# Attention edges: a drain between two chained sums in place of a semaphore's update and wait

## The chip, the cores and the metric

The kernel runs on one core of a Trainium2 chip. The metric is the device time of one execution in microseconds (us). The kernel before was run three times; the median is 8269.03 us.

## What is computed

A graph of 12500 nodes and 200000 edges, sorted by their target node, passes through an equivariant message layer and then through two graph attention layers. The change lies in the edge loop of the attention layers, which runs twice. What it computes, cut to the core:

```python
feat = (h @ W).reshape(n, H, F)                 # H = 4 heads, F = 64
e = leaky_relu(el[src] + er[dst], 0.2)
m = segment_max(e, dst)
ex = exp(e - m[dst])
denom = segment_sum(ex, dst)
a = ex / denom[dst]
out = segment_sum(feat[src] * a[:, :, None], dst)
```

Since the edges are sorted, a segment's sum is a running sum along the edges that starts anew where the target changes.

## The kernel before

Each of the 128 partitions holds a chunk of 1563 consecutive edges. The function `gat_edges` walks over them in blocks of 32 edges (`SBT`): 47 full blocks, and then the last two cut into four pieces of 16, 16, 15 and 12 edges (`ENDS`). So a layer has 51 pieces and the two layers 102. Three buffers `gb` (`B = 3`) hold the rows of a block: for each edge 256 features and the attention terms.

The engines work side by side and tell each other by semaphores.

- **GpSimd** (L1810) issues one indirect DMA for each edge index of a block, 32 a block, which fetches one row for each partition. Before a block it waits in `free`: for the store of the block that had the buffer, and until the block two before has got to its third wide product (L1898; `s_sum` with `back=2`).
- **VectorE** does the arithmetic in `body`. First come the small steps L1876 to L1904: the mask of the block, the attention score with its leaky ReLU, two scans for the segment's maximum, and, after ScalarE's exponential (L1837), the weights and the scan of the denominator. Then comes the chain: for each edge `t` the line L1910 makes `rows[t] = row[t-1] * same[t] + wv[t]`, a multiply and add of 128 x 256 values, in which `same[t]` is 1 where edge `t` has the target of the edge before and 0 otherwise. Each sum reads what the sum before it wrote. The products `wv` of feature and weight are made four edges at a time by L1898 (`weighted`), into two PSUM buffers in turn; the next four are issued behind the first sum of a group of four. I call such a group a quad.
- **SyncE** stores a finished block (L1782), once the last sum and ScalarE's copies of denominator and maximum (L1840) are there.

In the kernel before the order within VectorE is held by a semaphore of its own, `s_dv`. `own(ins)` lets an instruction raise it, `after(k)` lets the next one wait for it; it is cleared at the start of each block (L1875). In the chain every sum but the last raises it (`k_row = own(ins)`), and the next sum waits (`after(k_row)`); the first sum waits for the first product (`k_w`). Two other semaphores matter: `s_sum`, raised by each product from the third of a block on and by the block's last sum (GpSimd and SyncE wait for it), and `s_d`, `s_w`, `s_den` between VectorE and ScalarE.

Of the kernel before, what the change touches and what calls it, by code (L numbers as in the profile page):

```python
# [62 lines left out]
def bc(ap, dim, shape):  # L63
    return ap.unsqueeze(dim).to_broadcast(shape)
# [1662 lines left out]
def gat_edges(nc, q, n):  # L1727
# [13 lines left out]
    with ExitStack() as c:  # L1741
# [34 lines left out]
        with nc.Block(no_gpsimd_drain=True) as block:  # L1776
# [75 lines left out]
            @block.vector  # L1852
            def _(eng):
                def body(s, p, t0, t1, first, masks, arrived, before, behind, m_before):
                    m = t1 - t0
                    made = 0

                    def own(ins):
                        nonlocal made
                        made += 1  # L1860
                        ins.then_inc(s_dv, 1)
                        return made

                    def after(k):
                        eng.wait_ge(s_dv, k)

                    rows = gb[:, p, :, :]
                    here = bass.ds(first, m)
                    add_m, back_m, mul_m = masks
                    lead = lambda y: heads(y, m)[:, :, 0:1]  # L1870
                    carry = lambda y: heads(y, m_before)[:, :, m_before:m_before + 1]
                    x = heads(ee, m)[:, :, 1:]
                    eng.wait_ge(s_sum.sem, before)
                    eng.nop(nofuse=True)
                    eng.sem_clear(s_dv)  # L1875
                    eng.tensor_copy(same[:, 0:m], q.samep[:, here])  # L1876
                    eng.wait_ge(s_seg.sem, s_seg.at(s, back=1))
                    eng.tensor_copy(lead(ee), carry(mm_))
                    eng.wait_ge(*arrived)
                    k_el = own(eng.tensor_tensor(x, rows[:, t0:t1, D:FR].rearrange("p t h -> p h t"), held[:, :, here], ALU.add))  # L1880
                    after(k_el)
                    k_el = own(eng.scalar_tensor_tensor(x, x, 0.2, x, ALU.mult, ALU.max))
                    after(k_el)
                    k_fs = own(eng.tensor_tensor_scan(line(fs, m), add_m, line(ee, m), -BIG, ALU.add, ALU.max))
                    after(k_fs)
                    k_mm = own(eng.tensor_tensor_scan(line(mm_, m)[:, ::-1], back_m, line(fs, m)[:, ::-1], -BIG, ALU.add, ALU.max))
                    after(k_mm)
                    eng.tensor_tensor(heads(ee, m), heads(ee, m), heads(mm_, m), ALU.subtract).then_inc(s_d.sem, 1)  # L1888

                    eng.wait_ge(s_w.sem, s_w.at(s))  # L1890
                    eng.tensor_tensor(acc[:, :].rearrange("p (h c) -> p h c", c=C), behind.rearrange("p (h c) -> p h c", c=C),
                                      lead(ww).to_broadcast([P, H, C]), ALU.mult)

                    def weighted(k):
                        n = min(4, m - 4 * k)
                        f = rows[:, t0 + 4 * k:t0 + 4 * k + n, 0:D].rearrange("p t (h c) -> p t h c", c=C)
                        w = heads(ww, m)[:, :, 1 + 4 * k:1 + 4 * k + n].rearrange("p h t -> p t h")
                        return eng.tensor_tensor(wv[k % 2][:, 0:n, :].rearrange("p t (h c) -> p t h c", c=C), f, bc(w, 3, [P, n, H, C]), ALU.mult)  # L1898

                    k_w = own(weighted(0))  # L1900
                    after(k_w)
                    k_dn = own(eng.tensor_tensor(lead(ww), lead(ww), carry(dn), ALU.mult))
                    after(k_dn)
                    eng.tensor_tensor_scan(line(dn, m), mul_m, line(ww, m), 0.0, ALU.mult, ALU.add).then_inc(s_den.sem, 1)  # L1904
                    k_row = k_w
                    for t in range(m):
                        k, j = divmod(t, 4)
                        row = acc[:, :] if t == 0 else rows[:, t0 + t - 1, 0:D]
                        after(k_row)
                        ins = eng.scalar_tensor_tensor(rows[:, t0 + t, 0:D], row, same[:, t:t + 1], wv[k % 2][:, j, :], ALU.mult, ALU.add)  # L1910
                        if t == m - 1:
                            ins.then_inc(s_sum.sem, min(2, len(quads(t0, t1))))
                        else:
                            k_row = own(ins)
                        if j == 0 and 4 * (k + 1) < m:
                            if k == 0:
                                weighted(1)
                            else:
                                weighted(k + 1).then_inc(s_sum.sem, 1)

                eng.sem_inc(s_sum.sem, s_sum.base)
                eng.memset(gb[:, B - 1, SBT - 1, 0:D], 0.0)
                eng.memset(dn[:, :, :], 0.0)
                eng.memset(mm_[:, :, :], -BIG)
                for masks, (s, t0, t1) in zip(end_masks, ENDS):
                    m = t1 - t0
                    add, back, mul = (y[:, :].rearrange("p (h t) -> p h t", h=H) for y in masks)
                    flags = q.samep[:, s * SBT + t0:s * SBT + t1]
                    eng.memset(add[:, :, 0:1], -BIG).then_inc(s_mask, 1)
                    eng.memset(back[:, :, 0:1], -BIG).then_inc(s_mask, 1)  # L1930
                    eng.memset(mul[:, :, 0:1], 0.0).then_inc(s_mask, 1)
                    eng.tensor_copy(mul[:, :, 1:], bc(flags, 1, [P, H, m])).then_inc(s_mask, 1)
                    eng.tensor_scalar(add[:, :, 1:], bc(flags, 1, [P, H, m]), BIG, -BIG, ALU.mult, ALU.add).then_inc(s_mask, 1)
                    eng.tensor_scalar(back[:, :, 1:], bc(flags[:, ::-1], 1, [P, H, m]), BIG, -BIG, ALU.mult, ALU.add).then_inc(s_mask, 1)
                eng.wait_ge(s_ini, 16)
                eng.wait_ge(s_ch, 16)
                for x, e0 in enumerate(range(0, CE, SPAN)):
                    es = slice(e0, min(e0 + SPAN, CE))
                    for h in range(H):
                        first = ini[:, h:h + 1] if x == 0 else held[:, h, e0 - 1:e0]  # L1940
                        if x > 0:
                            eng.wait_ge(s_held, (x - 1) * H + h + 1)
                        eng.tensor_tensor_scan(held[:, h, es], q.samep[:, es], ch.rearrange("p (e h) -> p e h", h=H)[:, es, h], first, ALU.mult, ALU.add).then_inc(s_held, 1)
                eng.wait_ge(s_held, H * SPANS)
                def whole(i, p):
                    s = i * B + p
                    body(s, p, 0, SBT, s * SBT, [y[:, bass.ds(s * (H * W), H * W)] for y in (q.seg_add, q.seg_back, q.seg_mul)],
                         (s_g[p].sem, s_g[p].at(i)), s_sum.at(s, 0), gb[:, (p - 1) % B, SBT - 1, 0:D], SBT)

                with eng.Fori(0, LOOPS) as i:  # L1950
                    for p in range(B):
                        whole(i, p)
                for p in range(B - 1):
                    whole(LOOPS, p)
                eng.wait_ge(s_mask, 6 * len(ENDS))
                for x, (s, t0, t1) in enumerate(ENDS):
                    p = s % B
                    body(SB - 2 + x, p, t0, t1, s * SBT + t0, [y[:, :] for y in end_masks[x]],
                         (s_ge[x], 16 * (t1 - t0)), summed(x),
                         gb[:, p, t0 - 1, 0:D] if t0 else gb[:, (p - 1) % B, SBT - 1, 0:D], ENDS[x - 1][2] - ENDS[x - 1][1] if x else SBT)  # L1960
# [36 lines left out]
```

## Time and profile before

| what | us |
|---|---|
| median of 3 runs | 8269.03 |
| lowest and highest run | 8267.43, 8291.18 |
| the profiled execution, its time | 8222.85 |
| its span, first to last instruction | 8220.9 |
| VectorE busy | 5315.2 (65%) |
| GpSimd busy | 5491.2 (67%) |
| VectorE's sums of L1910, busy | 1450.0 |

The profile is taken from one execution. Busy time is that of an engine's own instructions; waits, register steps and DMA issues are not in it. The first layer's edge loop runs from about 3240 to 5490 us, the second's from about 5800 to 8050 us. DVE is VectorE, POOL is GpSimd, ACT is ScalarE. "Idle before" is the time in which an engine did nothing ahead of an instruction, and behind the arrow stands what ended it, as far as the semaphores' records tell ("remote" and "issue": nothing that the profile shows).

### The profile page before, as it was taken

How to read it: one execution, taken by the hardware profiler on the slowest of the kernel's cores; microseconds unless marked ns; L12 is line 12 of the kernel's file. 1: busy time of each engine (PE TensorE's matmuls, PEld its weight loads, DVE VectorE, ACT ScalarE, POOL GpSimd, SP SyncE). 2: the span in 40 equal slices, each digit the busy share in tenths (PEclk: the TensorE clock that was granted, in tenths of full speed). 3: DMA queues.
4: the chain of work that ended last, by engine and by line, in shares of the span. 5: the costliest groups of instructions: out<-in, count | busy, mean ns of one | idle time of the engine just before them, and what ended most of it. 6: DMA issues, size and time to landing. Idle time of an engine off the chain costs nothing. (4 is left out here: it accounts for less than half of the span.)

```text
span 8220.9 us, 58166 instructions
## 1 busy us (share of the span) xinstructions
PE 2470.7 (30%) x11337; PEld 1689.0 (21%) x11337; DVE 5315.2 (65%) x9727; ACT 2245.6 (27%) x5114; POOL 5491.2 (67%) x5324
## 2 busy tenths in 40 slices
PE   4777777777667676000000000005100000000000
PEld 4444444444444455000000000004000000000000
DVE  6777777777768777556556655663456556655666
ACT  3667666767667552000000000002000000000002
POOL 4777777767777646666666666647766666666664
PEclk8888988888888798555555555557555555555555
DMA  7555555555555547555555555543455555555556
GB/s 240 162 167 164 167 163 167 168 160 170 160 160 168 157 135 217 166 189 196 184 197 179 201 180 198 185 170 93 140 191 190 191 195 182 197 182 200 176 207 220
DMA packets 680849, 1466.14 MB, mean 178 GB/s; under 512 B 164313, under 2 KB 497566, under 8 KB 667420
## 3 DMA queue, kind: packets, MB, share of 16 engines
q0 software_dynamic: 250192, 671.13, 28.1%
q1 hardware_dynamic: 430540, 793.82, 27.2%
q14 instruction: 89, 0.73, 0.0%
q8 instruction: 28, 0.46, 0.0%
HBM read 752.61 MB, written 713.36 MB: 178 GB/s over the span
## 5 line engine op out<-in xcount | busy, mean ns | idle before, releaser
L1810 POOL DMA_INDIRECT gb_g<-table,ix_g x3126 | 2965.2, 949 | 1442.6 <-issue 938.1
L585 POOL DMA_INDIRECT gb<-table,src x1563 | 1897.1, 1214 | 679.5 <-issue 468.9
L1910 DVE SCALAR_TENSOR_TENSOR gb_g<-gb_g,same_g,wv 128x256 f32<-128x256 f32 x3024 | 1450.0, 479 | 1135.8 <-DVE gb_g L1910 471.3
L1096 PE MATMUL pm<-ident,tl 128*4 128x128 f32 x2 | 0.7, 372 | 4531.2 <-DMA tl<-sums 4531.2
L619 PE MATMUL po<-parts,sel 128*128 128x256 f32 x3930 | 1026.0, 411 | 501.3 <-ACT ost L685 353.5
L1837 ACT ACTIVATE ww<-ee 128x132 f32<-128x132 f32 (+3 forms) x102 | 28.5, 280 | 4030.2 <-DVE ee L1888 2811.7
L1898 DVE TENSOR_TENSOR wv<-gb_g,ww 128x1024 f32<-128x1024 f32 x782 | 955.2, 1221 | 0.0
L1096 PEld LDWEIGHTS pm<-ident,tl 128*4 128x4 f32 x2 | 0.2, 81 | 4532.1 <-DMA tl<-sums 4532.1
L619 PEld LDWEIGHTS po<-parts,sel 128*128 128x128 f32 x3930 | 762.8, 202 | 746.5 <-issue 478.1
L762 DVE TENSOR_TENSOR pt<-gb,pt 128x256 f32<-128x256 f32 x392 | 175.8, 449 | 546.4 <-ACT pt L679 414.8
L679 ACT ACTIVATE pt<-pt,sh 128x128 f32<-128x128 f32 x1568 | 436.8, 344 | 331.8 <-remote 175.2
L666 ACT ACTIVATE sq<-iota_f,behind 128x128 f32<-128x128 f32 x1568 | 503.1, 412 | 0.0
L609 PE MATMUL pt<-m,r 64*128 64x256 f32 x3136 | 452.6, 406 | 121.7 <-DVE parts L774 96.7
L685 ACT ACTIVATE ost<-po 128x1024 f32<-128x1024 f32 x393 | 403.1, 1026 | 295.9 <-remote 259.3
L742 DVE TENSOR_TENSOR dots<-gb,sh 128x768 f32<-128x768 f32 x392 | 381.1, 972 | 33.6 <-DMA gb<-table,src 32.1
L602 PE MATMUL pm<-r,m 128*128 128x512 f32 x784 | 389.7, 621 | 42.3 <-ACT r L661 31.6
L729 DVE TENSOR_TENSOR parts<-parts 128x768 f32<-128x768 f32 x393 | 384.9, 979 | 0.0
L766 DVE TENSOR_TENSOR parts<-pt,sh 128x768 f32<-128x768 f32 x392 | 382.7, 976 | 0.0
L769 DVE TENSOR_TENSOR parts<-gb,pt 128x768 f32<-128x768 f32 x392 | 380.8, 971 | 0.0
L609 PEld LDWEIGHTS pt<-m,r 64*128 64x128 f32 x3136 | 285.1, 189 | 401.5 <-issue 387.1
L661 ACT ACTIVATE r<-pm 128x1024 f32<-128x1024 f32 x294 | 301.4, 1025 | 199.0 <-issue 74.9
L774 DVE TENSOR_TENSOR parts<-gb,pt 128x512 f32<-128x512 f32 x392 | 276.6, 705 | 0.0
(302 smaller groups left out, 4208.3 us busy)
## 6 DMA issues: line engine op xcount, KB each, us to landing
sums<-gb_g SPq DMA_DIRECT2D x94, 4224.0 KB
sums<-ost SPq DMA_DIRECT2D x393, 512.0 KB
gb_g<-table,ix_g POOLq DMA_INDIRECT x3126
gb<-table,src POOLq DMA_INDIRECT x1563
table<-f SPq DMA_DIRECT2D x48, 520.0 KB
x<-in_x SPq DMA_DIRECT2D x50, 256.0 KB
at<-in_rbf SPq DMA_DIRECT2D x100, 128.0 KB
hT_d<-hT SPq DMA_DIRECT2D x49, 256.0 KB
```

The lines of the kernel that those rows point to most:

```text
L585: eng.indirect_dma_start(out=gb[:, group(k), half(k) + j, 0:4, :].rearrange("p a c -> p (a c)"), out_offset=None, in_=q.table0[:, :], in_o ...
L602: ins = eng.matmul(pm[:, g, :], m23[:, n, :], r[n][:, g, :], start=True, stop=True)
L609: ins = eng.matmul(pt[k % 2][:, 2 * h + j, :], r3[hid(h), pair(k), group(k) % 2, j0:j0 + P], m4[hid(h), :], start=True, stop=True)
L619: ins = eng.matmul(po[:, j, :], sel[:, k % 4, j, :], y.rearrange("p a c -> p (a c)"), start=y is parted[0], stop=y is parted[-1])
L666: ins = eng.activation(sq[:, 4 * (k % 2) + j, :], q.iota_f[:, :], ACT.Square, scale=2.0, bias=behind2[:, bass.ds(i * (4 * K) + (4 * (k - 1 ...
L679: ins = eng.activation(w, w, ACT.Copy, scale=sh[:, group(k), 4 * ((k - 1) % 2) + j, 0:1])
L685: eng.activation(ost[:, k % 4, :, :], po[:, :, :], ACT.Copy).then_inc(s_ev.sem, 1)
L729: eng.tensor_tensor(m, m, tmp[:, k % 4, 0:BOTH, :, :], ALU.add).then_inc(s_msg.sem, 1)
L766: eng.tensor_tensor(msg[:, b, :, 1:4, :], bc(w[:, :, 1, :], 2, [P, 4, 3, C]), s1, ALU.mult)
L1810: eng.indirect_dma_start(out=gb[:, p, j, 0:FR], out_offset=None, in_=q.table1[:, :], in_offset=bass.IndirectOffsetOnAxis(ap=ix[:, s * SBT ...
L1898: return eng.tensor_tensor(wv[k % 2][:, 0:n, :].rearrange("p t (h c) -> p t h c", c=C), f, bc(w, 3, [P, n, H, C]), ALU.mult)
L1910: ins = eng.scalar_tensor_tensor(rows[:, t0 + t, 0:D], row, same[:, t:t + 1], wv[k % 2][:, j, :], ALU.mult, ALU.add)
```

## The change

In the chain, the wait for `s_dv` in front of each sum goes, and the update of `s_dv` by each sum but the last goes with it. In place of them VectorE executes a `drain` in front of each sum, the first included. The update of `s_sum` by the last sum stays, and so do the waits and updates of the steps ahead of the chain and those of the products.

```diff
                     eng.tensor_tensor_scan(line(dn, m), mul_m, line(ww, m), 0.0, ALU.mult, ALU.add).then_inc(s_den.sem, 1)
-                    k_row = k_w
                     for t in range(m):
                         k, j = divmod(t, 4)
                         row = acc[:, :] if t == 0 else rows[:, t0 + t - 1, 0:D]
-                        after(k_row)
+                        eng.drain()
                         ins = eng.scalar_tensor_tensor(rows[:, t0 + t, 0:D], row, same[:, t:t + 1], wv[k % 2][:, j, :], ALU.mult, ALU.add)
                         if t == m - 1:
                             ins.then_inc(s_sum.sem, min(2, len(quads(t0, t1))))
-                        else:
-                            k_row = own(ins)
                         if j == 0 and 4 * (k + 1) < m:
```

## Rows read from the trace of the kernel before

**Rows 1.** Costliest groups: line, engine, tiles, count | busy us, mean ns | idle before, releaser.
```profile
L1810 POOL DMA_INDIRECT gb_g<-table,ix_g x3126 | 2965.2, 949 | 1442.6 <-issue 938.1
L1910 DVE SCALAR_TENSOR_TENSOR gb_g<-gb_g,same_g,wv 128x256 f32<-128x256 f32 x3024 | 1450.0, 479 | 1135.8 <-DVE gb_g L1910 471.3
```

**Rows 2.** Who waited for whom, whole run: us in total, times, longest us.
```profile
POOL gb_g L1810 <- DVE wv L1898: 504.4, 47, 19.9
```

**Rows 3.** Windows, L1876 alone (one per block): stretch, us, DVE busy (count), clock, DMA.
```profile
3440.00:5387.70 1947.70, 8.34 (x43) 0.50 0.56 190
```

**Rows 4.** Windows, the same stretch, L1810 alone: GpSimd's gathers (count).
```profile
3440.00:5387.70 1947.70, 1309.67 (x1384) 0.50 0.56 190
```

**Rows 5.** Timeline, quick stretch: start us, us, engine line op tiles count [idle before, releaser].
```profile
4616.41 0.18 DVE L1876 COPY same_g<-samep 128x32 f32 x1 [0.28 <-DVE gb_g L1910]
...
4617.07 0.29 DVE L1882 SCALAR_TENSOR_TENSOR ee<-ee 128x128 f32<-128x128 f32 x1
4617.50 0.44 DVE L1884 TENSOR_TENSOR_SCAN fs<-seg_add,ee 128x132 f32<-128x132 f32 x1
...
4621.41 0.45 DVE L1910 SCALAR_TENSOR_TENSOR gb_g<-acc_g,same_g,wv 128x256 f32<-128x256 f32 x1
...
4621.78 1.22 DVE L1898 TENSOR_TENSOR wv<-gb_g,ww 128x1024 f32<-128x1024 f32 x1
...
4622.91 2.02 DVE L1910 SCALAR_TENSOR_TENSOR gb_g<-gb_g,same_g,wv 128x256 f32<-128x256 f32 x4
4623.11 0.95 POOL L1810 DMA_INDIRECT gb_g<-table,ix_g  x1 [0.30 <-issue]
...
4624.85 1.22 DVE L1898 TENSOR_TENSOR wv<-gb_g,ww 128x1024 f32<-128x1024 f32 x1
```

**Rows 6.** Timeline of VectorE, slow stretch: a quad, and the next block's start.
```profile
6843.37 1.22 DVE L1898 TENSOR_TENSOR wv<-gb_g,ww 128x1024 f32<-128x1024 f32 x1
6844.50 0.47 DVE L1910 SCALAR_TENSOR_TENSOR gb_g<-gb_g,same_g,wv 128x256 f32<-128x256 f32 x1
6847.18 0.48 DVE L1910 SCALAR_TENSOR_TENSOR gb_g<-gb_g,same_g,wv 128x256 f32<-128x256 f32 x1 [2.20 <-remote]
6848.58 0.48 DVE L1910 SCALAR_TENSOR_TENSOR gb_g<-gb_g,same_g,wv 128x256 f32<-128x256 f32 x1 [0.92 <-DVE gb_g L1910]
...
6850.37 1.22 DVE L1898 TENSOR_TENSOR wv<-gb_g,ww 128x1024 f32<-128x1024 f32 x1
...
6863.52 0.22 DVE L1876 COPY same_g<-samep 128x32 f32 x1 [1.79 <-remote]
...
6868.18 0.29 DVE L1882 SCALAR_TENSOR_TENSOR ee<-ee 128x128 f32<-128x128 f32 x1 [4.04 <-remote]
...
6877.71 0.46 DVE L1910 SCALAR_TENSOR_TENSOR gb_g<-acc_g,same_g,wv 128x256 f32<-128x256 f32 x1
```

**Rows 7.** Timeline of VectorE: a wholly slow block, two of its sums, the next block.
```profile
3330.24 0.18 DVE L1876 COPY same_g<-samep 128x32 f32 x1 [1.79 <-remote]
...
3347.49 0.48 DVE L1910 SCALAR_TENSOR_TENSOR gb_g<-gb_g,same_g,wv 128x256 f32<-128x256 f32 x1 [1.47 <-issue]
3349.60 0.48 DVE L1910 SCALAR_TENSOR_TENSOR gb_g<-gb_g,same_g,wv 128x256 f32<-128x256 f32 x1 [1.64 <-issue]
...
3400.23 0.18 DVE L1876 COPY same_g<-samep 128x32 f32 x1 [1.79 <-remote]
```

**Rows 8.** Timeline: three sums, and the gather that ends a pause of GpSimd.
```profile
4594.58 1.51 DVE L1910 SCALAR_TENSOR_TENSOR gb_g<-gb_g,same_g,wv 128x256 f32<-128x256 f32 x3 [1.62 <-remote]
...
4597.98 0.94 POOL L1810 DMA_INDIRECT gb_g<-table,ix_g  x1 [11.11 <-DVE wv L1898]
```

**Rows 9.** Timeline, end of the first layer's edges: last gather, last piece, last sums.
```profile
5443.34 0.95 POOL L1810 DMA_INDIRECT gb_g<-table,ix_g  x1 [0.30 <-issue]
...
5478.09 0.17 DVE L1876 COPY same_g<-samep 128x12 f32<-128x12 f32 x1 [0.19 <-DVE gb_g L1910]
...
5486.41 3.64 DVE L1910 SCALAR_TENSOR_TENSOR gb_g<-gb_g,same_g,wv 128x256 f32<-128x256 f32 x7
```

## The prediction

> **What bounds the kernel now.** Start with the page's costliest groups [rows 1]. The gathers of the attention edges (L1810, GpSimd) head it: 3126 of 949 ns, each behind 938.1 / 3126 = 0.30 us of issue, so one per 1.25 us. The chained sums of L1910, the line that the change is about, are second by waiting: 1450 us busy and 1135.8 us of idle time in front of them. Which of the two engines sets the time of a block? The waits of GpSimd answer [rows 2]: 47 times it stood still for VectorE's L1898 (the gate that frees a gather buffer), 504.4 us in all. So in the edge loops VectorE is late and GpSimd waits for it.
>
> Next, a block's length. In the settled stretch of the first layer 43 blocks of 32 edges pass in 1947.70 us [rows 3], 45.30 us each, a pair 90.6. GpSimd needs 32 x 1.25 = 40.0 us for a block's gathers. In the same stretch its 1384 gathers [rows 4] make 1384 x 1.25 = 1730 us; the rest, 218 us, is those waits.
>
> Now the timeline of VectorE, in two places. In the quick one [rows 5] a block needs 5.00 us from its first copy (4616.41) to its first sum (4621.41); from one product of L1898 to the next, a quad, 3.07 us (4621.78 to 4624.85); four sums run in 2.02, one per 0.51 for 0.48 of work, so a semaphore's update and wait cost about 0.04 us. A whole block at this pace is 5.0 + 7 x 3.07 + 2.05 for the last quad + 0.28 to the next block = 28.8 us.
>
> The held one [rows 6] has the same instructions with the same durations, and a quad takes 7.00 us (6843.37 to 6850.37). Sums that wait for the sum before start 1.40 us apart (6847.18, 6848.58). After the quad's first wide product the next sum starts at 6844.50, and the one that waits for it only at 6847.18, 2.68 later. I read it so: each *update* of a semaphore by VectorE takes effect 1.40 us after the one before it; a quad makes five (four sums, one product), 5 x 1.40 = 7.00; the product's own update stands in front of that of the sum at 6844.50. What carries no wait starts at once (the product at 6843.37, 0.40 behind its sum). A block wholly of this kind is 70.0 us (3330.24 to 3400.23, two first copies [rows 7]), of which 14.19 pass before its first sum (6863.52 to 6877.71 [rows 6]). If a pair has x quick blocks and 2 - x held ones, 28.8x + 70.0(2 - x) = 90.6, so x = 1.2. The held stretch ends while GpSimd pauses: at 4594.58 three sums run in 1.51 us, 3.4 us before the gather that ends an 11.11 us pause [rows 8].
>
> **The change, part by part.** *Taken away:* in each block 31 updates of the chain's own semaphore and the waits for them, 3126 - 102 = 3024 in all (one sum of each of the 102 pieces tells another semaphore and keeps that). *Kept:* the updates ahead of the chain, that of each product from the third on, that of the last sum. *Added:* 3126 drains. *Moved:* nothing, no DMA and no queue.
>
> What does a drain cost? The trace has none. Bounds, by the gap from an instruction's end to the start of one that needs it: from below 0.04 us, a wait that the engine itself holds (2.02 for four [rows 5]); from above 0.92 us, the gap of the held chain [rows 6]. Between lies the row most like it, one where the sequencer holds the next instruction back: L1884 starts 0.14 us behind L1882's end (4617.07 + 0.29 to 4617.50 [rows 5]), with a register step between; the first copy of a block waits 0.28 behind three such steps. I take g = 0.14, since a drain is one step of the sequencer, and keep both ends. A drain costs cover too: the sum behind a product starts 1.13 us after it now, before the product's 1.22 are over, and then has to wait them out; likewise the first sum behind L1904.
>
> In the quick stretch the removed update and wait are worth 0.04 us a sum [rows 5], in the held one 0.92 [rows 6]. The Trainium skill (VectorE: DVE Perf Modes, The DRAIN you can't avoid) holds that a semaphore behind every VectorE operation costs nothing extra over one behind the last, and advises saving operations, not semaphores. The quick stretch agrees, the held one does not; by the rule the sum below would be nought, 8269 us, no update being worth its removal.
>
> A quad becomes 0.40 + 1.22 + 3 x 0.48 + 4g = 3.06 + 4g = 3.62 us, the last 4 x 0.62 = 2.48, the first sum 0.2 later. A quick block: 5.2 + 7 x 3.62 + 2.48 + 0.28 = 33.3 us, that is 28.8 + 32g, 4.5 more than now. A held block, if the sums no longer wait for updates: 14.19 + 0.2 + 27.8 of chain + 1.8 to the next = 44.0, that is 39.5 + 32g, 26 less than now. A pair in today's mixture: 1.2 x 33.3 + 0.8 x 44.0 = 75.2 us, under GpSimd's 80.0. So GpSimd's gathers become the bound, and VectorE's dearer drains hide below them, with 4.8 us of cover per pair; it is gone at g = 0.22, and all gain is at g = 0.38 (66.2 + 64g = 90.6).
>
> The sum, against the profiled execution (8222.85 us, span 8220.9, so 2 us around it): GpSimd's 504.4 us of waits go. What is late next is the landing of gathers behind a block's store, and a held block's 44.0 against 40.0; I give back 0.6 us per block for them, 94 x 0.6 = 56. The end of each layer shortens: today the last sum ends 46.7 us after the last gather starts (5443.34 to 5490.05 [rows 9]), since VectorE is behind; then what remains is the last piece (12 us, 5478.09 to 5490.05, and 2 for its drains) and part of the piece before, about 26: 20 off, twice, 40. Together -504 + 56 - 40 = -488: 7735 us for a profiled execution. The runs' median, 8269.03, lies 46 us above the profiled one; I carry that over: 7780 us.
>
> **Rivals.**
>
> *The drain waits for the product's held update as well (7870 to 8100 us).* For it: the held update belongs to an instruction that a drain must see finished. Against it: VectorE runs on past it today (the sum at 6844.50 [rows 6]). A held block then pays 7 x 1.40 = 9.8 us more, 53.8. In today's mixture a pair is 40.0 + 43.0 = 83.0 us, 3.8 per block under today's, 94 x 3.8 = 357 and the ends 40: 7870. If half of the blocks are held, a pair is 87.1, 1.75 per block, 164 us: 8100.
>
> *Slower (8520 to 8690 us): the 1.40 us belong to an instruction's completion, not to its update.* A drain waits for completion, so the held quad keeps its 7.00 us or more, and quick ones pay the drains. The pair is 1.2 x 33.3 + 0.8 x 70.0 = 96.0, or 99.6 with the drains' 4.5 us in the held block too: 5.4 to 9.0 us over today's 90.6, times 47 pairs, 254 to 423 us. It decides from a mean gap of 0.38 us per drain. For it: the copies that open a block update nothing, and yet the first wait behind them takes 4.04 us (6868.18 [rows 6]), room for three completions. Against it: the second product of a block carries no update. Behind it the sums at 3347.49 and 3349.60 [rows 7] stand 2.11 us apart, where a completed product and a completed sum would make 2 x 1.40 = 2.80 after the first one's release.
>
> *Nothing gained (8269 us).* The holding moves to other waits, say the eight dependent steps ahead of the chain, until a pair is 90 us again: they would have to take 14 us more per held block than their 14.19. Against it: in the wholly held block they take no more than 14.2 already. The Trainium skill's rule of the free semaphore (VectorE: DVE Perf Modes, The DRAIN you can't avoid) ends here too.
>
> **How the numbers follow.** Forecast, GpSimd bound: 0.59, its own range 7700 (no leftover lag and nearly all of the tail) to 7870. Held product: 0.20, 7870 to 8240 with a dearer drain. No change: 0.05. Slower: 0.16. A measurement of this kernel tells about 0.3%, 25 us, from no change. Faster 0.79, same 0.05, slower 0.16. The range is 7700 to 8250 us: it takes in the first two cases and leaves out the slower one, and of the fourth all but its edge: 0.2. It is wide because g is unknown between 0.04 and 0.92, and g = 0.22 with a held product (88.1 us a pair) already gives 8110.
>
> **What would show it.** Right: GpSimd's waits for L1898 nearly gone; gathers 1.25 us apart through a whole layer; blocks of about 40 us; sums 0.6 to 0.65 us apart nearly everywhere, and no pitch of 1.40 in the chain. The steps ahead of the chain may still take 14 us at times. Held product: a gap of about 1.4 us behind each L1898 in places, none between sums. Slower: 1.40 us or more between sums, with drains between. The forecast is wrong if the drains' gap is over 0.22 us in the mean, or if GpSimd still pauses every other block.

## The result, and the profile after

The kernel with drains takes 8476.36 us (median of 4 runs, 8460.35 to 8492.50), the kernel before in the same comparison 8270.01 (4 runs). The ratio is 1.0248, 95% interval [1.0225, 1.0271]: 206 us slower. The forecast was 7780, the range 7700 to 8250. The side came out wrong; of the rivals it was the slower one, by a smaller amount than the 8520 to 8690 us that stood there.

The profiled execution took 8465.79 us (span 8463.8), 242.9 more than that of before. Its costliest groups answer to [rows 1]: the gathers and the sums are as long as they were (950 and 480 ns), and both engines wait more.

```profile
L1810 POOL DMA_INDIRECT gb_g<-table,ix_g x3126 | 2970.5, 950 | 1623.6 <-issue 938.2
L1909 DVE SCALAR_TENSOR_TENSOR gb_g<-gb_g,same_g,wv 128x256 f32<-128x256 f32 x3024 | 1451.9, 480 | 1272.0 <-issue 1133.8
```

The waits of GpSimd answer to [rows 2], the window over 43 blocks to [rows 3]. The waits rose by 181 us, from 504.4; a block by 2.15, from 45.30 to 2040.20 / 43 = 47.45, and 94 x 2.15 = 202 us.

```profile
POOL gb_g L1810 <- DVE wv L1898: 685.4, 50, 20.1
```

```profile
3484.90:5525.10 2040.20, 7.79 (x43) 0.50 0.54 182
```

Layer by layer: from the first copy of an edge loop to the end of its last sum the kernel before needs 2222.0 and 2219.7 us, the changed one 2320.5 and 2319.9, 198.7 more in all. Another 42.8 of the profiled difference lie ahead of the change: the first edge block starts at 3310.88 instead of 3268.08 us, before any edge loop has run. The kernels of the experiments start it at 3304 to 3368. So the profiled execution of before had an early start; it reads as most of the 46 us between that execution and the median (not shown, since it is one execution), and lies outside the edge loops.

Now VectorE in a quick quad, which answers to [rows 5] (timeline: start, us, instruction, count):

```profile
4604.98 1.22 DVE L1898 TENSOR_TENSOR wv<-gb_g,ww 128x1024 f32<-128x1024 f32 x1
4606.30 2.14 DVE L1909 SCALAR_TENSOR_TENSOR gb_g<-gb_g,same_g,wv 128x256 f32<-128x256 f32 x4
4608.35 1.22 DVE L1898 TENSOR_TENSOR wv<-gb_g,ww 128x1024 f32<-128x1024 f32 x1
```

From product to product it is 3.37 us, 0.30 more. Four sums take 2.14: one per (2.14 - 0.48) / 3 = 0.553 us, so a drain leaves a gap of 0.07 where the semaphore left 0.03. That is 0.04 three times. The rest is overlap: the first sum now starts 0.10 us behind the product's end (4606.20), while in [rows 5] it started 0.09 ahead of it.

And in a held stretch, answering to [rows 6]:

```profile
4641.18 1.22 DVE L1898 TENSOR_TENSOR wv<-gb_g,ww 128x1024 f32<-128x1024 f32 x1
4643.58 0.48 DVE L1909 SCALAR_TENSOR_TENSOR gb_g<-gb_g,same_g,wv 128x256 f32<-128x256 f32 x1 [1.18 <-issue]
4644.99 0.48 DVE L1909 SCALAR_TENSOR_TENSOR gb_g<-gb_g,same_g,wv 128x256 f32<-128x256 f32 x1 [0.93 <-issue]
4646.38 0.48 DVE L1909 SCALAR_TENSOR_TENSOR gb_g<-gb_g,same_g,wv 128x256 f32<-128x256 f32 x1 [0.91 <-issue]
4647.78 0.48 DVE L1909 SCALAR_TENSOR_TENSOR gb_g<-gb_g,same_g,wv 128x256 f32<-128x256 f32 x1 [0.92 <-issue]
4648.18 1.22 DVE L1898 TENSOR_TENSOR wv<-gb_g,ww 128x1024 f32<-128x1024 f32 x1
```

The sums stand 1.40 us apart with no update among them, the releaser column names no semaphore any more, and the quad takes 7.00 us (4641.18 to 4648.18), to the digit what it took before. A wholly held block is 70.0 us from first copy to first copy, as in [rows 7] (both are the second block of a layer; the later blocks are part quick, part held):

```profile
3373.19 0.18 DVE L1876 COPY same_g<-samep 128x32 f32 x1 [0.29 <-issue]
...
3394.11 0.48 DVE L1909 SCALAR_TENSOR_TENSOR gb_g<-gb_g,same_g,wv 128x256 f32<-128x256 f32 x1 [0.92 <-issue]
3394.81 0.48 DVE L1909 SCALAR_TENSOR_TENSOR gb_g<-gb_g,same_g,wv 128x256 f32<-128x256 f32 x1 [0.22 <-issue]
...
3443.18 0.36 DVE L1876 COPY same_g<-samep 128x32 f32 x1 [0.28 <-issue]
```

A block has 50 instructions of VectorE: 32 sums, 8 products and 10 steps ahead of the chain. 50 x 1.40 = 70.0. Single sums come 0.70 us early, as the two in the middle do, or late; the sum of the block is 70.0 all the same.

### The profile page after: what moved, and what is told of

Same layout as the page of the kernel before. It is cut to its first block and busy times, and to the rows that moved or that the text cites. A ratio compares the mean times of both kernels' runs of the same rounds, so it can differ in the third digit from the quotient of the medians.

```text
span 8463.8 us, 61190 instructions
## 1 busy us (share of the span) xinstructions
PE 2491.3 (29%) x11337; PEld 1702.5 (20%) x11337; DVE 5387.6 (64%) x9727; ACT 2246.5 (27%) x5114; POOL 5477.5 (65%) x5324
## 5 line engine op out<-in xcount | busy, mean ns | idle before, releaser
L1810 POOL DMA_INDIRECT gb_g<-table,ix_g x3126 | 2970.5, 950 | 1623.6 <-issue 938.2
L585 POOL DMA_INDIRECT gb<-table,src x1563 | 1877.3, 1201 | 714.8 <-issue 468.4
L1909 DVE SCALAR_TENSOR_TENSOR gb_g<-gb_g,same_g,wv 128x256 f32<-128x256 f32 x3024 | 1451.9, 480 | 1272.0 <-issue 1133.8
```

The costliest lines, as they stand in the source:

```text
L585: eng.indirect_dma_start(out=gb[:, group(k), half(k) + j, 0:4, :].rearrange("p a c -> p (a c)"), out_offset=None, in_=q.table0[:, :], in_o ...
L1810: eng.indirect_dma_start(out=gb[:, p, j, 0:FR], out_offset=None, in_=q.table1[:, :], in_offset=bass.IndirectOffsetOnAxis(ap=ix[:, s * SBT ...
```

## The experiments

The theory after the result: in a held stretch each *instruction* of VectorE completes 1.40 us after the one before, whether or not it updates a semaphore; a wait for its semaphore and a drain both wait for that completion. Rivals: only updates are spaced; a store of SyncE makes the stretch; or something else that the 1.40 us count. Ratios are to the kernel before, run beside the experiment on the same chip, since its median differed from chip to chip: 8282.73 us beside e1, e2, e4 and e5, 8347.90 beside e3, e6, e7 and e8, 8386.35 beside e9 and e10. The expectations count from about 8270, so a time is compared with them by its ratio. "Mean block" is taken from the profile, as in [rows 3].

**One more instruction per quad, without an update** (e1_filler, on the kernel before):

```diff
                         if j == 0 and 4 * (k + 1) < m:
...
+                        if j == 2:
+                            eng.memset(spot[:, k % 2:k % 2 + 1], 0.0)
```

> The kernel before, with one more VectorE instruction per quad in the chain: a memset of one value per partition into a tile that nobody reads. It waits for nothing, updates no semaphore, and takes about 0.06 us. Theory (count): in the held stretch every VectorE instruction, whatever it is, is completed 1.40 us after the one before it. A full block has 50 of them, and 50 x 1.40 = 70.0 us is just what the wholly held block took. With 58 a held block takes 81.2 us, a held quad 6 x 1.40 = 8.40 instead of 7.00; a pair 1.2 x 29.3 + 0.8 x 81.2 = 100 us, so 94 x 4.7 = 445 us more: about 8715 us. Rival (update): only updates of semaphores are spaced; the memset makes none, a held quad stays at 7.0 to 7.1, at most 0.5 us per block: 8270 to 8320 us.

Measured: 8513.01 us, ratio 1.0282 [1.0246, 1.0318]. The timeline of a held quad of this kernel:

```profile
3618.03 1.22 DVE L1899 TENSOR_TENSOR wv<-gb_g,ww 128x1024 f32<-128x1024 f32 x1
...
3621.83 0.48 DVE L1911 SCALAR_TENSOR_TENSOR gb_g<-gb_g,same_g,wv 128x256 f32<-128x256 f32 x1 [2.20 <-remote]
3622.26 0.06 DVE L1917 MEMSET spot_g<- 128x1 f32 x1
3623.23 0.48 DVE L1911 SCALAR_TENSOR_TENSOR gb_g<-gb_g,same_g,wv 128x256 f32<-128x256 f32 x1 [0.91 <-DVE gb_g L1911]
3626.03 0.48 DVE L1911 SCALAR_TENSOR_TENSOR gb_g<-gb_g,same_g,wv 128x256 f32<-128x256 f32 x1 [2.32 <-issue]
3626.43 1.22 DVE L1899 TENSOR_TENSOR wv<-gb_g,ww 128x1024 f32<-128x1024 f32 x1
```

A write of one value per partition, 0.06 us long, with no update and nobody waiting for it, costs a whole 1.40: the two sums around its completion stand 2.80 apart (3623.23, 3626.03), the quad takes 8.40 = 6 x 1.40. The theory that only updates are spaced would have left 7.00; it falls. The total is about half of what the count gave: the mean block is 48.28 us, which is 1.27 quick blocks in a pair (of 29.3 and 81.2 us) instead of 1.2. A whole block of 81.2 us was not seen: the longest take 77.0 and 77.7, and the last sums of the former run quick, in a pause of GpSimd.

**Semaphores and drains together** (e2_both, on the kernel before: the drain is added, update and wait stay):

```diff
                         after(k_row)
+                        eng.drain()
```

> The kernel before with the drains added and nothing taken away: each sum waits for the semaphore and then for the drain. Theory (count): the removed updates and waits were worth nothing, all of the change is the drains' price in the quick stretch, so this takes what the changed kernel takes: 8476 us within 25, quick quad 3.4 us, held quad 7.0. Rival (update): the removal gained something and the drains cost more than it; then this is slower than the changed kernel by what was gained, 50 us or more: above 8525 us.

Measured: 8468.45 us, ratio 1.0219 [1.0189, 1.0248], against 1.0248 without the semaphores. Its quick quad:

```profile
3652.59 1.22 DVE L1898 TENSOR_TENSOR wv<-gb_g,ww 128x1024 f32<-128x1024 f32 x1
3653.90 2.21 DVE L1911 SCALAR_TENSOR_TENSOR gb_g<-gb_g,same_g,wv 128x256 f32<-128x256 f32 x4
3656.03 1.22 DVE L1898 TENSOR_TENSOR wv<-gb_g,ww 128x1024 f32<-128x1024 f32 x1
```

The quad is 3.44 us, 0.07 above that of the change. So beside the drains what the change takes away is worth at most 0.07 us a quad and nothing in the total; the whole loss is what it adds.

**The drain behind a product replaced by its wait** (e3_mixed, on the kernel after; 24 drains a block stay):

```diff
-                        eng.drain()
+                        if j == 1:
+                            after(k_row)
+                        else:
+                            eng.drain()
```

> The changed kernel, but the sum behind a product (the second of each quad) waits by semaphore for the first sum of its quad, as before, so it need not wait until the product is out of VectorE; 8 of a block's 32 drains go. Theory: the 2.15 us that a block gained by the change are the price of drains in the quick stretch, and it has two parts: 0.07 us more per drain, 32 x 0.07 = 2.2 less what a semaphore's wait cost (0.04), and in each quad some 0.17 us in which sum and product no longer overlap. A quick quad goes from 3.38 to 3.2 us, 1.3 us per block at most: 94 x 1.2 = 110 us less than the changed kernel, 8340 to 8400 us. Rival: the overlap was worth nothing, since the time goes in the held stretch: 8450 to 8500 us.

Measured: 8440.16 us, ratio 1.0113 [1.0070, 1.0157], so about half of the change's loss is gone. The expected 8340 to 8400 is 1.0085 to 1.0157 of 8270, and the ratio lies in it. Its quick quad:

```profile
4604.60 1.22 DVE L1898 TENSOR_TENSOR wv<-gb_g,ww 128x1024 f32<-128x1024 f32 x1
4605.73 2.14 DVE L1913 SCALAR_TENSOR_TENSOR gb_g<-gb_g,same_g,wv 128x256 f32<-128x256 f32 x4
4607.79 1.22 DVE L1898 TENSOR_TENSOR wv<-gb_g,ww 128x1024 f32<-128x1024 f32 x1
```

The sum starts 1.13 us behind the product again, inside its 1.22, and the quad is 3.19, 0.18 less than with the drain there. The overlap is the larger half of the drains' price.

**The store in four pieces** (e4_split_store, on the kernel before), for the rival that a block's store makes the stretch:

```diff
-                    eng.wait_ge(s_sum.sem, s_sum.at(s))
-                    eng.dma_start(out_v[:, s * SBT:(s + 1) * SBT, :], gb[:, p, :, :]).then_inc(s_st[p].sem, 16)
+                    for k in range(4):
+                        eng.wait_ge(s_sum.sem, s_sum.at(s, 2 * (k + 1)))
+                        eng.dma_start(out_v[:, s * SBT + 8 * k:s * SBT + 8 * (k + 1), :], gb[:, p, 8 * k:8 * (k + 1), :]).then_inc(s_st[p].sem, 16)
```

> The kernel before, with the store of a block cut into four of 8 edges, each issued once its sums are there. What starts the held stretch? Theory (burst): the block's store of 4.2 MB keeps the gathers back for some 12 us, and their landing in one burst starts it (in the settled stretch it begins 13 us after each store's issue). Four stores of 1 MB keep them back for 3 us each; no held stretch, GpSimd is the bound with 40.0 us per block: 7750 to 7850 us. Rival (fill): it needs no burst, only VectorE instructions while gathers land at their full rate, as in the first block, where it began at 3304.7 us before any store of a block. Then blocks stay near 45 us: 8200 to 8350 us.

Measured: 8400.34 us, ratio 1.0151 [1.0124, 1.0177]. In its profile, which is of its longest run (8443.39 us), held blocks stay, of the same length:

```profile
3391.12 0.18 DVE L1877 COPY same_g<-samep 128x32 f32 x1 [1.79 <-issue]
...
3461.11 0.18 DVE L1877 COPY same_g<-samep 128x32 f32 x1 [1.78 <-remote]
```

A store of a whole block isn't needed to hold VectorE. The time was above both expectations, with a mean block of 46.73 us in that profile.

**Fewer instructions** (e5_wide on the kernel after, e6_wide_sem with semaphores as before): products of 16 edges, written over the rows that they read, so 2 a block in place of 8, and 44 instructions.

```diff
-        wv = [pb(c, f"wv{k}_{n}", [P, 4, D]) for k in range(2)]
+        G = 16
...
-                        n = min(4, m - 4 * k)
+                        n = min(G, m - G * k)
...
-                        return eng.tensor_tensor(wv[k % 2][:, 0:n, :].rearrange("p t (h c) -> p t h c", c=C), f, bc(w, 3, [P, n, H, C]), ALU.mult)
+                        return eng.tensor_tensor(f, f, bc(w, 3, [P, n, H, C]), ALU.mult)
```

> The changed kernel with fewer VectorE instructions: the products are made in place in the rows, 16 edges at a time, so two wide products take the place of eight, and each sum reads both operands from SBUF. 44 instructions in a block for 50. The fourth sum of each quad tells GpSimd. Theory (count): a held block takes 44 x 1.40 = 61.6 us, a quick one about 31.2; a pair 1.2 x 31.2 + 0.8 x 61.6 = 86.7 us for 90.6 of before: 94 x 1.95 = 183 us less, about 8090 us. Rival (work): the time goes with the work of VectorE, which is the same here: as the changed kernel, 8450 to 8500 us. Rival (operands): two operands in SBUF keep GpSimd's gathers waiting: gathers further than 1.25 us apart, slower than 8476 us.

> The kernel before with its semaphores and no drain, but with products made in place, 16 edges at a time: 44 VectorE instructions in a block for 50; the fourth sum of a quad raises the semaphore that GpSimd waits for, and the sum behind it waits for that one. Theory (count): a held block takes 44 x 1.40 = 61.6 us for 70.0. The same 44 instructions with drains gave 44.84 us per block in the mean; without the drains' 2.15 us that is 42.7, 2.6 under the kernel before: 94 x 2.6 = 245 us less, about 8030 us. Rival (work): VectorE's work decides; it is no less here than before: 8250 to 8310 us.

Measured: e5_wide 8283.81 us, ratio 1.0014 [0.9995, 1.0034], so 2.3% under the kernel after (1.0014 to 1.0248); e6_wide_sem 8264.93, ratio 0.9901 [0.9872, 0.9930]. First copies of held blocks, of e5_wide and then of e6_wide_sem:

```profile
3421.62 0.18 DVE L1876 COPY same_g<-samep 128x32 f32 x1 [0.28 <-issue]
...
3483.27 0.18 DVE L1876 COPY same_g<-samep 128x32 f32 x1 [0.34 <-issue]
```

```profile
3591.58 0.18 DVE L1876 COPY same_g<-samep 128x32 f32 x1 [1.86 <-remote]
...
3653.21 0.21 DVE L1876 COPY same_g<-samep 128x32 f32 x1 [1.86 <-remote]
...
3714.81 0.18 DVE L1876 COPY same_g<-samep 128x32 f32 x1 [1.86 <-remote]
```

A held block takes 61.6 us with drains and with semaphores: 44 x 1.40. The count of instructions is confirmed to a tenth. The totals are not: 8090 and 8030 were expected. The e6 lines show one reason: held blocks follow each other, where before a quick stretch followed each. The page and the waits of e5_wide show a second:

```profile
L1810 POOL DMA_INDIRECT gb_g<-table,ix_g x3126 | 3131.3, 1002 | 1318.0 <-issue 940.2
```

```profile
POOL gb_g L1810 <- DVE gb_g L1909: 377.8, 43, 17.9
```

GpSimd waits 308 us less than in the kernel after, but its gathers have grown from 950 to 1002 ns, 161 us over 3126.

**VectorE with 22 instructions a block** (e7_scan, edited from the kernel after; its semaphores are back and no drain is left): one scan for 8 edges in place of 8 sums; ScalarE spreads the mask ahead of it and copies the rows behind it.

```diff
-                        ins = eng.scalar_tensor_tensor(rows[:, t0 + t, 0:D], row, same[:, t:t + 1], wv[k % 2][:, j, :], ALU.mult, ALU.add)
+                        k_row = own(eng.scalar_tensor_tensor(wT[:, :, 0], row, same[:, ts.start:ts.start + 1], wT[:, :, 0], ALU.mult, ALU.add))
...
+                        eng.tensor_tensor_scan(flat(oT[g % 2]), flat(mk), flat(wT), 0.0, ALU.mult, ALU.add).then_inc(s_sc.sem, 1)
```

> Far fewer VectorE instructions with the same result: products of 8 edges go to PSUM with the edge as the fast dimension, one sum carries the row before into the first of the 8, and one scan over 2048 values makes the 8 running sums; ScalarE expands the mask for it and copies the rows back. 22 VectorE instructions in a block for 50, of about 34 us of work. Theory (count): 22 x 1.40 = 31 us, so the held stretch can no longer hold a block beyond its own work, and GpSimd's 40.0 us per block becomes the bound: no pauses, 94 x 5 = 470 us less, 7780 to 7880 us. Rival (shared): ScalarE's 8 further instructions of 2 us or the scan's rate over PSUM keep VectorE above 42 us per block: 8000 us or more.

Measured: 8221.79 us, ratio 0.9833 [0.9801, 0.9864], the fastest of those with all of the gathers, but not the 7780 to 7880. The groups of its page, then GpSimd's timeline:

```profile
L1816 POOL DMA_INDIRECT gb_g<-table,ix_g x3126 | 3298.7, 1055 | 1025.2 <-issue 1023.7
...
L1936 DVE TENSOR_TENSOR_SCAN oT<-mk,wT 128x2048 f32<-128x2048 bf16 x392 | 1733.0, 4421 | 41.1 <-DVE wT L1931 0.5
```

```profile
4683.92 1.10 POOL L1816 DMA_INDIRECT gb_g<-table,ix_g  x1 [0.30 <-issue]
4685.32 1.10 POOL L1816 DMA_INDIRECT gb_g<-table,ix_g  x1 [0.30 <-issue]
4686.72 1.12 POOL L1816 DMA_INDIRECT gb_g<-table,ix_g  x1 [0.30 <-issue]
```

GpSimd waits for nobody (1023.7 of its 1025.2 us are issue), so the gathers are the bound, as the forecast wanted them. But now a third of them are the ones 1.40 us apart: of 3125 distances between their starts in its trace 1550 lie at 1.24 to 1.27 us, 1032 at 1.38 to 1.42, nearly all others above. Over the run one takes (3298.7 + 1023.7) / 3126 = 1.383 us, times 32 is 44.2 us a block; the mean block is 44.51. The 40.0 us of 32 gathers at 1.25 [rows 3, 4] were not a bound that stays when VectorE's count falls to 22. Why these gathers slow down isn't shown: the edit also moves the copying of the rows to ScalarE and changes what each engine reads.

**Instructions of another engine** (e8_act, on the kernel before): 24 tiny ones of ScalarE per block.

```diff
+                    for k in range(24):
+                        eng.activation(spot[:, k:k + 1], q.eps_c[:, :], ACT.Copy)
```

> The kernel before with 24 further instructions of ScalarE in each block, behind its copies of denominator and maximum: copies of one value per partition into a tile that nobody reads, some 5 us of work on an engine that is idle there; nobody waits for them. Theory (private): the 1.40 us belong to VectorE's own completions, ScalarE's instructions don't matter: 8250 to 8310 us. Rival (shared): completions of all engines pass one place; where ScalarE's copies ended in a held stretch before, two sums stood 2.11 us apart in place of 1.40, 0.70 for each. Then 24 x 0.70 = 17 us per held block, 0.4 of them: 94 x 6.7 = 630 us more, up to 8900 us.

Measured: 8359.76 us, ratio 1.0008 [0.9987, 1.0028]. ScalarE's instructions don't count; VectorE's do (e1_filler).

**The gathers: bytes or number** (e9_small: as many, each of 16 bytes; e10_half: half as many, of full length; both on the kernel before, one run each):

```diff
-                    eng.indirect_dma_start(out=gb[:, p, j, 0:FR], out_offset=None, in_=q.table1[:, :],
+                    eng.indirect_dma_start(out=gb[:, p, j, D:FR], out_offset=None, in_=q.er_d,
```

```diff
-                    for j in range(SBT):
+                    for j in range(0, SBT, 2):
```

> The kernel before, with the same number of gathers, but each fetches 16 bytes per partition from a small table in place of 1040; the features of the rows stay what they were, so the output is not the reference's. Does the held stretch depend on the bytes that the gathers move? Theory (number): it depends on the gathers' number, not their size: there are still stretches in which sums stand 1.40 us apart, and blocks take 44 to 46 us. Rival (bytes): with hardly any bytes landing VectorE is never held, GpSimd is the bound: blocks of 40.0 us, about 7780 us.

> The kernel before, but a full block gathers only every second of its 32 rows; the others stay what they were, so the output is not the reference's. GpSimd needs 20 us per block and pauses for the rest. Theory (gathers): VectorE is held only while gathers come without a pause; now each block has one, so blocks take VectorE's own time, 29 to 34 us, 94 x 13 = 1200 us less: about 7000 us. Rival (own): the holding comes from VectorE's own instructions, 50 in a block, whatever GpSimd does: blocks stay near 45 us, 8270 us.

Measured: 8383.14 and 6766.71 us beside 8386.35. With 16 bytes a gather VectorE is held as ever (timeline of e9_small, then its gathers on the page):

```profile
3564.35 0.48 DVE L1910 SCALAR_TENSOR_TENSOR gb_g<-gb_g,same_g,wv 128x256 f32<-128x256 f32 x1 [2.20 <-issue]
3565.75 0.48 DVE L1910 SCALAR_TENSOR_TENSOR gb_g<-gb_g,same_g,wv 128x256 f32<-128x256 f32 x1 [0.92 <-DVE gb_g L1910]
3567.15 0.48 DVE L1910 SCALAR_TENSOR_TENSOR gb_g<-gb_g,same_g,wv 128x256 f32<-128x256 f32 x1 [0.92 <-DVE gb_g L1910]
```

```profile
L1810 POOL DMA_INDIRECT gb_g<-er_d,ix_g x3126 | 2958.6, 946 | 1519.1 <-issue 937.7
```

With half of the gathers GpSimd pauses in each block (for the store), and the settled blocks are quick (first copies, then GpSimd's waits):

```profile
3428.83 0.18 DVE L1876 COPY same_g<-samep 128x32 f32 x1 [0.28 <-issue]
...
3457.72 0.18 DVE L1876 COPY same_g<-samep 128x32 f32 x1 [0.34 <-DVE gb_g L1910]
...
3486.65 0.18 DVE L1876 COPY same_g<-samep 128x32 f32 x1 [0.28 <-issue]
```

```profile
POOL gb_g L1810 <- DMA sums<-gb_g: 777.8, 85, 11.7
```

28.9 us a block, as the quick block of 28.8 that the prediction put together. At the end of its layers this kernel has a stream without a pause: the last four pieces gather all of their rows, 59 gathers from 4684.65 to 4757.22. There VectorE is held again, from about 4727 to 4765 (the gather that starts the stream, then two of the sums):

```profile
4684.65 0.94 POOL L1810 DMA_INDIRECT gb_g<-table,ix_g  x1 [9.53 <-DMA sums<-gb_g]
...
4755.23 0.48 DVE L1910 SCALAR_TENSOR_TENSOR gb_g<-gb_g,same_g,wv 128x256 f32<-128x256 f32 x1 [2.20 <-remote]
4756.63 0.48 DVE L1910 SCALAR_TENSOR_TENSOR gb_g<-gb_g,same_g,wv 128x256 f32<-128x256 f32 x1 [0.92 <-DVE gb_g L1910]
```

So the held stretches come with a stream of gathers that runs on without a pause, whatever its bytes, and go where the stream pauses.

## Why the prediction was wrong

**The step that failed** is "A held block, if the sums no longer wait for updates: ... = 44.0". It rested on the reading that each update of a semaphore takes effect 1.40 us after the one before. What is spaced in a held stretch is the completion of every VectorE instruction (e1_filler, e5_wide, e6_wide_sem); a drain waits for that as the semaphore did, and the held block stayed at 70.0 us (after), 70.0 (e4_split_store, semaphores), 61.6 with 44 instructions. The 26 us of gain per held block never were there.

**The clue that was passed over.** [rows 7] give 70.0 us for a wholly held block, and that is 50 x 1.40 when every instruction is counted. Counting updates alone falls short: the two copies that open a block, the product of L1891 and the block's second product update nothing, so it has 46 updates, and 46 x 1.40 = 64.4. Against completion the prediction set one pitch, 2.11 us where two completions make 2.80. One odd pitch was weighed against the sum of a block; the sum was the better witness. The 2.11 itself stays unexplained; it is one of those single completions that come 0.70 early.

**The slower rival** had the mechanism, "the 1.40 us belong to an instruction's completion, not to its update", with two terms too large. The drain's gap is 0.07 us, not 0.14; a quick quad 3.37, not 3.62; so a quick block is 28.8 + 8 x 0.30 = 31.2 by estimate, not 33.3. And the held block takes none of the drains' 4.5. With these its pair is 1.2 x 31.2 + 0.8 x 70.0 = 93.4, 2.8 over 90.6, 132 us in 47 pairs. The pair measured 2 x 47.45 = 94.9, which is x = 1.16 quick blocks instead of 1.2; those 1.5 us are another 70 us. That it "decides from a mean gap of 0.38 us" was wrong too: with the held block unchanged, any gap above that of the semaphore costs.

**The held product** had its gap behind the product: 1.18 us, from 4642.40 to 4643.58. But it put none between the sums, where 0.91 to 0.93 stand. **Nothing gained**: by e2_both the removed waits and updates are worth nothing that the total shows. There the Trainium skill (VectorE: DVE Perf Modes, The DRAIN you can't avoid) was right against the prediction's 0.92 us; but the 8269 us left out what the added drains cost.

**The cover.** The drains were to hide below GpSimd's 80.0 us a pair. VectorE stayed the late engine in both kinds of stretch, so nothing hid the drains of the quick ones: by the windows 202 us, of the 206 measured. **The end of the layer** was to lose 20 us and gained 6.7: the last sum ends 53.4 us after the last gather's start (5577.93 to 5631.38), against 46.7 in [rows 9].

**The signs.** The forecast was to be wrong "if GpSimd still pauses every other block". It pauses 50 times for 94 blocks. The other sign, a mean gap of the drains over 0.22 us, is there too: 1272.0 us of idle time before 3024 sums is 0.42 each. The sign named for the slower case, 1.40 us between sums with drains between, is the timeline shown above.

**Left open.** What the completions share with the gathers, and why 1.40 us; each run comes with a recorded span, so no run here could tell whether the recording itself takes part. What starts a held stretch isn't settled, but it needs no store: the first one of the kernel before begins at 3304.7 us, ahead of the first store of a block at 3330.0. Besides, in the settled rhythm it comes mostly 13 to 16 us after a store there and 10 to 11 in the kernel after. The distance from the end of GpSimd's pause is steadier: 29 to 35 us in both kernels. In the kernel after, for one, a pause ends at 3559.26 and the sums fall out of their quick pace some 31 us later:

```profile
3559.26 0.95 POOL L1810 DMA_INDIRECT gb_g<-table,ix_g  x1 [14.61 <-DVE wv L1898]
...
3590.81 0.48 DVE L1909 SCALAR_TENSOR_TENSOR gb_g<-gb_g,same_g,wv 128x256 f32<-128x256 f32 x1 [0.51 <-issue]
```

In the two kernels with 44 instructions a block that distance is mostly 63 to 74 us, and with the split store 37 to 66. It reads as if something fills while gathers stream and VectorE runs quick, and empties in a pause; the bursts of e10_half, 16 gathers in 20 us, end before that. What fills isn't shown, and no run was made to test it. How the blend of quick and held blocks follows from the two: every total that assumed it constant missed (e1_filler, e5_wide, e6_wide_sem). Kernels that leave out the stores, or space the gathers apart, were not tried.

## What to carry to other kernels

Before a wait is taken out, ask whether what stands in its place waits for the same event; a drain waits for the completion that the semaphore reports, and on top of that it ends the overlap of independent instructions, here a product and the next sum. Where instructions stand at a pitch that their length doesn't explain, divide the length of a whole block by the pitch and compare with the count of instructions, of updates and of waits, before believing one odd gap. Then save what is counted: 44 instructions in place of 50 were worth 1.0% on the kernel with semaphores and 2.3% on the one with drains, which loses less overlap too with fewer products; beside drains the semaphores were worth nothing. (That edit also moved the products from PSUM to SBUF, so not all of its gain need be the count's.)

## What the runs showed of the hardware

- Beside a steady stream of GpSimd's indirect gathers, one per 1.25 us, VectorE falls into stretches in which its instructions complete 1.40 us apart in the mean, from a memset of 0.06 us to a product of 1.22 us: 70.0 us for 50 of them, 61.6 for 44. Gathers of 16 bytes do the same (e9_small); 24 more ScalarE instructions a block change nothing (1.0008).
- With VectorE at 22 instructions a block (e7_scan) a third of the gathers stand 1.40 us apart; one takes 1.383 in the mean. In the settled stretch of the first layer no kernel with all the gathers had a mean block under 44.5 us.
- A drain of VectorE between two dependent sums leaves a gap of 0.07 us in a quick stretch, and costs 0.18 to 0.19 more behind a product that would have overlapped.
- The drains' own records run from 294 to 3392 ns, median 1323: they hold the wait for the engine, and are no price. The row is that of the source line, all of the kernel after:

```profile
L1908 DVEq DRAIN  x3126: 294/1323/3392, 3333.4 to 8294.1; - x196
```
